# Row maxima spread through the vector engine's step, and the odd query stack copied on GpSimd

## What is computed

```
h = layernorm(x) * (1 + ca) + sa                 # ca, sa, ... from silu(c) @ wmod, one row per batch
a = h + proj(windowed_attention(layernorm(h)))   # 16 heads of 8, windows of 64 tokens that step by 32
a = a + mlp(layernorm(a))                        # 128 -> 512 -> 128 with gelu
x = x + ga * a
h = layernorm(x) * (1 + cb) + sb
x = x + gb * sum_e weight_e(h) * expert_e(h)     # 8 experts, silu(h Wg) * (h Wu) @ Wd
```

## Time and profile before

| | |
|---|---|
| median of 3 runs | 341.74 us (339.88 to 345.77) |
| the profiled execution | 342.37 us, its span 340.6 us |
| mean granted TensorE clock | 0.843 of full speed |
| busy share of the span | PE 83%, PEld 65%, DVE 66%, ACT 41%, POOL 23% |
| attention, 8 steps | about 54 to 217 us, some 20.5 us each |
| stack reads | 48 DMAs of 216 KB, median 4.8 us from issue to landing |

### The profile page before, as it was taken

How to read it: one execution, slowest core, us unless ns; L and a number is a source line. 1 busy time by engine, 2 the same in 40 slices (tenths; PEclk the granted TensorE clock), 3 DMA queues, 4 the chain that set the end, 5 groups by cost and what they waited for, 6 DMA issues and landing times.

```text
span 340.6 us, 10357 instructions
## 1 busy us (share of the span) xinstructions
PE 283.2 (83%) x4168; PEld 222.6 (65%) x4168; DVE 225.3 (66%) x634; ACT 141.0 (41%) x282; POOL 77.3 (23%) x116
## 2 busy tenths in 40 slices
PE   4855479599797898969798999887899989999992
PEld 2423356487675666747687787565697778878992
DVE  7564664645858368363745626498857898798986
ACT  1354136328364372635226235554537216624220
POOL 5453240311405015000101110125540024003020
PEclk9995559659789696997659556999979999999999
DMA  5109652286617346172610350000000000100001
GB/s 179 46 0 219 148 121 70 81 192 145 153 51 161 105 96 162 44 168 75 134 29 6 89 172 3 0 2 0 0 2 1 0 2 0 32 2 31 2 32 32
DMA packets 21902, 23.71 MB, mean 70 GB/s; under 512 B 3296, under 2 KB 18528, under 8 KB 21856
## 3 DMA queue, kind: packets, MB, share of 16 engines
q1 hardware_dynamic: 21856, 23.06, 27.4%
HBM read 14.67 MB, written 8.13 MB: 67 GB/s over the span
## 4 chain that ended last, share of the span: by engine, by line
PE 46%; DVE 18%; issue 9%; DMA 9%; SPq 9%; ACT 6%; POOL 3%; DVEq 0%; ACTq 0%; POOLq 0%
PE bank L655 6%; SPq L285 5%; PE bank L450 4%; PE bank L407 4%; DVE xh L1032 4%; DMA qst<-stack_scratch 3%; PE bank L440 3%; PE bank L392 3%; PE bank L430 3%; PE bank L637 3%; PE bank L371 3%; PE bank L639 3%; PE bank L638 3%; DMA qst<-mt 3%; DVE acc L1371 2%
## 5 line engine op out<-in xcount | busy, mean ns | idle before, releaser
L1073 DVE TENSOR_REDUCE nm<-bank 128x8 f32<-128x512 f32 x64 | 43.3, 689 | 29.6 <-PE bank L392 29.5
L740 ACT ACTIVATE prob<-bank 128x512 f32<-128x512 f32 x64 | 36.4, 599 | 28.0 <-PE bank L407 27.6
L878 POOL TENSOR_TENSOR rs<-ve,mhalf 128x2 f32<-128x2 f32 (+1 forms) x24 | 19.8, 827 | 122.6 <-DVE ve L1029 115.7
L392 PE MATMUL bank<-kst,qst 48*64 48x64 bf16 x1024 | 32.0, 211 | 9.3 <-issue 4.0
L392 PEld LDWEIGHTS bank<-kst,qst 48*64 48x64 bf16 x1024 | 25.1, 123 | 18.8 <-issue 13.1
L830 ACT ACTIVATE sg<-bank 128x512 f32<-128x512 f32 x32 | 18.9, 601 | 43.6 <-PE bank L639 42.1
L655 PEld LDWEIGHTS bank<-wds,hh 128*128 128x128 f32 x256 | 32.3, 191 | 7.0 <-issue 5.3
L655 PE MATMUL bank<-wds,hh 128*128 128x128 f32 x256 | 33.7, 277 | 2.7 <-DVE acc L1371 2.3
L407 PE MATMUL bank<-qst,kst 50*64 50x64 bf16 x1024 | 30.2, 210 | 5.2 <-DMA qst<-mt 4.7
L1371 DVE SCALAR_TENSOR_TENSOR acc<-bank,rt,acc 128x128 f32<-128x128 f32 x112 | 32.6, 341 | 1.2
L430 PE MATMUL bank<-prob,vb 128*32 128x64 f32 x1024 | 27.3, 255 | 6.8 <-issue 4.2
(11 more groups left out here) (140 smaller groups left out, 517.5 us busy)
## 6 DMA issues: line engine op xcount, KB each, us to landing
qst<-stack_scratch SPq DMA_DIRECT2D x32, 216.0 KB, 4.8
stack_scratch<-parts SPq DMA_DIRECT2D x16, 216.0 KB, 2.5
kst<-stack_scratch SPq DMA_DIRECT2D x16, 216.0 KB, 4.9
stack_scratch<-parts SPq DMA_DIRECT2D x16, 144.0 KB, 2.4
stack_scratch<-parts SPq DMA_DIRECT2D x16, 72.0 KB, 3.0
qst<-mt SPq DMA_DIRECT2D x64, 4.0 KB
out_x<-fin SPq DMA_DIRECT2D x4, 256.0 KB, 2.3
xs<-in_x SPq DMA_DIRECT2D x1, 896.0 KB, 7.3
```

The source lines that it names most:

```text
L392: m = pe.matmul(psa[g % 2][WIN * half:WIN * half + WIN, WIN * h2:WIN * h2 + WIN], qst[n][eo][rows_, h2, at:at + WIN], kst[n][rows_, h2, at ...
L740: act.activation(prob[g // 2 % 2][:, :, g % 2, :], psb[g % 2][:].rearrange("p (h q) -> p h q", h=H2), ACT.Exp).then_inc(exp_done, 1)
L1073: dve.tensor_reduce(nm[:, g, :], psa[g % 2][:].rearrange("p (h k) -> p h k", h=H2), AX_X, ALU.max, negate=True).then_inc(max_done, 1)
```

## The change

Three edits. The maxima are placed at other points of DVE's step, and with them ln_b and copy_mt(b + 1, 0). The second read of the query stack is taken out, and GpSimd copies the even stack's columns to the odd stack instead (`copy_odd`), with a semaphore of its own; scores_a of groups 0 to 3 waits for four DMAs and that of groups 4 to 7 for the copy. The copy covers 112 partitions, also those between the two halves, so DVE zeroes 32 partitions of each even query stack once at the start (three more memsets of the same shape as the six of `kst`).

```diff
@@ sync, read_stacks
-                for k, stack, written in ((0, qst[n][0], q_written), (1, kst[n], k_written),
-                                          (0, qst[n][1], q_written)):
+                for k, stack, written in ((0, qst[n][0], q_written), (1, kst[n], k_written)):
@@ sync, start
-            sp.wait_ge(ones_ready, after(ones_ready, 2 * DEEP))
+            sp.wait_ge(ones_ready, after(ones_ready, 3 * DEEP))
@@ tensor, scores_a
-                pe.wait_ge(stack_ready, after(stack_ready, 96 * (b + 1)))
+                if g < 4:
+                    pe.wait_ge(stack_ready, after(stack_ready, 64 * (b + 1)))
+                else:
+                    pe.wait_ge(odd_ready, after(odd_ready, b + 1))
@@ gpsimd
+            def copy_odd(b):
+
+                pool.wait_ge(stack_ready, after(stack_ready, 64 * (b + 1)))
+                even, odd = [qst[b % DEEP][eo][0:64 + ROWS, :, LINE - S:LINE] for eo in range(2)]
+                pool.tensor_copy(odd, even).then_inc(odd_ready, 1)
...
             copy_x1v(1)
+            copy_odd(0)
             cut_m(0, 0)
@@ gpsimd, step(b)
                 if b + 1 < B:
                     cut_m(b + 1, 0)
+                if b == 0:
+                    copy_odd(1)
...
                     second_root_x(b + 4)
+                if 0 < b < B - 2:
+                    copy_odd(b + 2)
                 if b + 1 < B:
                     cut_m(b + 1, 1)
+                if b == 0:
+                    copy_odd(2)
@@ vector, start
                     dve.memset(kst[n][64 * par + 32:64 * par + 64].bitcast(F32), TWO_ONES).then_inc(ones_ready, 1)
+                dve.memset(qst[n][0][32:64].bitcast(F32), 0.0).then_inc(ones_ready, 1)
@@ vector, step(b)
                 maxima_next(2)
+                if norm:
+                    ln_b(b + 4)
                 maxima_next(3)
                 if group is not None:
                     ln2_stats(group)
                 normalise(b, 0)
-                if norm:
-                    ln_b(b + 4)
+                if ahead:
+                    copy_mt(b + 1, 0)
+                maxima_next(4)
                 if prep:
                     cut_qk(b + 3, 0)
-                if ahead:
-                    copy_mt(b + 1, 0)
+                maxima_next(5)
                 if prep:
                     cut_qk(b + 3, 1)
                 if group is not None:
                     normed_tokens(group)
-                maxima_next(4)
+                maxima_next(6)
                 if not ahead:
                     gate(GA)
                 if norm:
                     ln_c(b + 4)
-                maxima_next(5)
-                maxima_next(6)
                 maxima_next(7)
```

More of the change, by code:

```diff
@@ L197, in build @@
         stack_ready = sem("stack_ready")
+        odd_ready = sem("odd_ready")
         v_done, v_ready = sem("v_done"), sem("v_ready")
```

## The result

| | before | after |
|---|---|---|
| median of the runs | 342.35 us (4 runs, 339.88 to 345.77) | 352.69 us (4 runs, 350.10 to 355.14) |
| profiled execution, its span | 342.37, 340.6 us | 355.14, 353.3 us |
| mean granted TensorE clock there | 0.843 | 0.808 |
| step 0 begins (first copy_mt of a step) | 54.69 us | 58.75 us |
| seven steps, to the same copy of step 7 | 146.3 us | 154.3 us |

The ratio of the times is 1.0364, with a 95% interval from 1.0295 to 1.0433: the change made the kernel slower, by 10.3 us between the medians and by some 12 us by the ratio, where I had forecast 338 us with a range of 332 to 345.

What follows compares the result with a forecast made beforehand. It took the attention as a PE program with holes, neither PE-bound nor DMA-bound. Start +2.5 and steps 1 to 4 -6.4 made -3.9 us on the profiled 342.37, so 338.5, or 338 us against the median; range 332 to 345.

Steps and rivals of the forecast that it cites:

- the costing of copy_odd: POOL's copy taken as 2.4 us, between second root and cut_m(b + 1, 1), hidden from transpose_m with 2.1 us left.
- Rival 2: PE's clock stays at 2.4 GHz without the holes of steps 1 to 4: 5 us shorter, 333 us; chance 0.22.
- The start: Before step 0: three more memsets, partly offset by an earlier first stack; net +2.5 us, ends +3.9 and +1.5.
- +3.9: At the start: three more memsets of 1.31 us each delay DVE's first dependent instruction by 3.9 us.
- -1.4: At the start: fewer reads let PE begin scores_a(0, 0) 2.4 us sooner, of which 1.4 us come back at m0.
- Steps 1 to 4: Earlier m4, maxima's rows and code block close PE's holes: gains 1.1, 2.0, 1.2 and 2.1 us, sum -6.4 us.
- The reads and the code: probs_v's "issue" holes are code queued behind stack reads; four reads bring it 2.2 us sooner, holes under 1 us.
- rival 1: "Issue" holes not tied to the reads: step 2 gains 1.0 us, step 4 nothing, 341 us; chance 0.2.
- it does not bind: Step 2: DVE keeps pace, normalise(b, 1) from 112.1 against 114.41, 2.3 us sooner, within a gain of about 2.0.
- Step 0: No gain; copy_odd(1) delays scores_a(1, 4) by 2.4 us, under PE's 3.35 us stall for ACT, which waits for write_parts.
- Rival 3: POOL late: copy takes 5.3 us, delaying steps 0 to 3; 344 us, decisive from 4.5 us a copy; chance 0.08.
- Rival 4: The start costs its full 3.9 us and the steps give 3 only: 342 to 343 us; chance 0.1.

Runs made afterwards that it cites:

- e11: e9 plus, on GpSimd where copy_odd had stood, same-shape copies that no other engine waits for; 348.41 us, ratio 1.0269 to the kernel before.
- e5: Changed kernel with the copies of steps 1 to 5 moved behind cut_m(b + 1, 1) and made to wait for ctxn; 340.02 us, ratio 1.0001 to the kernel before.
- e7: Changed kernel with copy_odd made by ScalarE in its idle stretches instead of GpSimd; 335.58 us, no ratio.
- e9: Changed kernel with copy_odd on ScalarE and the three added memsets in VectorE's idle places, more rounds than e8; 333.56 us, ratio 0.9875 to the kernel before.
- e1: Kernel before with only DVE's new order, keeping six reads a batch and six memsets; 340.52 us, ratio 0.9972.
- e2: Changed kernel with DVE's old order put back, keeping the GpSimd copy, four reads and added memsets; 345.32 us, no ratio.
- e12: Changed kernel with 22 matmuls on ones in place of 5 ahead of gather_context in steps 1 to 4; 343.91 us, ratio 1.0128 to the kernel before.
- e3: Kernel before with only the three more memsets added at DVE's head; 346.39 us, ratio 1.0108.
- e4: Changed kernel with its three added memsets moved from the head into DVE's idle places; 349.57 us, ratio 1.0199 to the kernel before.
- e8: Changed kernel with copy_odd on ScalarE and the three added memsets in VectorE's idle places; 335.75 us, no ratio.
- e10: e9 with DVE's old order put back; 338.65 us (328.94 to 352.64, 12 runs), no ratio.
- e6: Changed kernel with every GpSimd copy of batches 3 to 7 made twice in the same place; 352.87 us, ratio 1.044 to the kernel before.

## Why the prediction was wrong, point by point

**The step that failed** is the costing of copy_odd: "So it is hidden with 2.1 us left." I asked only how late POOL would be. The copy's length was over-estimated on the safe side (1.89 us, where I took 2.4 from a range of 1.8 to 5.3), cut_m followed it at once, and no transpose_m waited for it. But while it ran, it held DVE's instructions between SBUF operands, and one of these, fac, stands on the path from turn_sums to gather_context. My own working had both at the same moment, "112.1 to 114.5" for the copy and "normalise(b, 1) from 112.1", and I did not put the two lines side by side. I had even seen a DVE cast go from 0.46 to 0.78 us beside POOL and applied that factor to the copy, the wrong side: the one that starts later is the one that is held, and it is held to the end. Shown by e11 (the copy's presence alone costs it), e5 (place) and e7 to e9 (another engine). e1 and e2 show the order's part: by itself it costs nothing, but it brought fac of steps 1 to 3 under the copy.

The Trainium skill, "SBUF — State Buffer", section "Who interferes with whom", states this as a rule: GpSimd and VectorE share one pair of ports as an exclusive lock, which an instruction keeps for its whole length, and of VectorE's instructions those in a two-port mode need it, and so do those with two SBUF inputs when GpSimd's instruction reads SBUF, as this copy does. The traces agree with it: fac and qkr (two SBUF inputs) were held to the copy's end, the copy and the maximum out of PSUM were not. Section 8 of the Trainium skill, "GPSIMD Engine Reference", which the prediction cites, names the same two kinds of VectorE instruction as in contention with GpSimd; the prediction kept only the one with both ports, took the harm to fall on both, and did not look for one with two SBUF inputs behind ve.

**The size of it: the clock.** Rival 2 had the clock as a thing to gain when holes close. The holes I named did close, all of them; that a new hole of 2.9 us at another place would put a whole step at 1.2 GHz was not in any case. Its size is known only roughly. PE's busy time for the same matmuls is 5.4 us higher after the change, and in e12 it is 5.0 us lower again, with 68 matmuls more. The whole effect of e12 is about 8 of the 12 us, from ratios of 1.0364 and 1.0128 whose intervals just touch (1.0295 and 1.0311), and it has step 5 in it, which the added matmuls do not explain. So 5 us are the clock as far as shown, and what is over stays open.

**The start.** "+3.9" was right for DVE's first dependent instruction (3.7). "-1.4" was right as far as PE goes (2.8 us of the 3.7 came back before scores_a(0, 0), 2.4 were forecast), and failed on DVE for the same reason as above: copy_odd(0) begins at 39.32, held x1h until 41.29 and with it m0, which in the earlier trace rows had waited for PE. The sum at step 0 was +4.1 and not +2.5; of it the memsets alone have 1.95 (e3), and without them at the head it is gone (e4, -0.9).

**Steps 1 to 4.** m4 next to copy_mt, no stall before scores_a 6: right, in the changed kernel and e1. **The reads and the code**: right as far as tested. The holes stand at fixed instructions: that of step 4 with 9 matmuls of its probs_v left in the kernel before, e1, e3 and e7, that of step 2 with 17 left in the kernel before, e3, e8 and e9, whatever their length. This fits the reading as a boundary of code and no wait. With six reads the hole in step 4 is 2.75, 2.75 and 2.47 us (before, e1, e3), with four 0.55 (e7) or none (changed kernel, e2), so rival 1's "step 4 nothing" falls. But the reads are not all of it: step 2's hole went in e1 with six reads, e12 has 1.45 and 2.03 us with four, and the 1.14 us of step 7 in the changed kernel, over the 1 us that I had set as a sign, come behind other DMA traffic (share 0.94 from 212 to 214 us). Ahead of e12's 2.03 us the DMA share was 0.15 only (154 to 156 us). So what sets the length of such a hole stays open, and I had priced it by the end of the reads alone. But -6.4 us was the sum of four closed holes, as if nothing stood close behind them. In e1 the same PE program ran into waits for the maxima's rows and for ctxn, of 1.41 and 1.19 us, and gained nothing; step 2's "it does not bind" was wrong even without a copy. Only e9 against e10 hints that the order pays once the reads are four.

**Step 0.** I had copy_odd(1) hidden under PE's stall for ACT. It was. PE waited 2.00 us for the copy and then 2.95 us more for ACT's parts, where it had waited 3.35, but the end of this wait is set by ACT, and ACT was late by itself. ACT in order of time, step 0 before:

```profile
62.73 0.50 ACT L716 ACTIVATE qk<-bank,bqs 128x288 f32<-128x288 f32 x1 [4.42 <-DMA stack_scratch<-parts]
```

After:

```profile
68.46 0.50 ACT L719 ACTIVATE qk<-bank,bqs 128x288 f32<-128x288 f32 x1 [6.10 <-DMA stack_scratch<-parts]
```

Against the first copy_mt of the step, ACT goes on 1.7 us later than before, and PE's transposes come 1.7 us later too. It waits for the landing of write_parts, which comes 3.1 us behind the last issue where it came 1.6 behind it. The copy on GpSimd is not shown as its cause: e10, with no copy there, has 3.1 as well, and e11, with one, 2.1. So 1.7 of the step's 2.3 us stay open.

**Rivals 3 and 4** were the ones on the side of slower. Rival 3 had the copy's place right and the victim wrong: it made cut_m late at over 4.5 us a copy, and at 1.89 us it was out of play. Rival 4 had a start of 3.9 us (4.1 measured), but still with a gain of 3 in the steps. To more than 348.6 us I had given 0.04.

**What stays open.** In step 5 scores_b waits 3.33 us for the maxima's rows (1.82 before); e9 has 1.54 there and e12 0.97. SP issued those rows from 171.22 us and the stack reads behind them; no run took this wait apart.

## What to carry to other kernels

Before work is moved to GpSimd, list what VectorE does in that same stretch: each of its instructions between SBUF operands may have to wait for the whole of one GpSimd instruction, whatever its own size, so a short one on the path to TensorE can cost as much as the longest thing GpSimd runs (0.19 us became 1.78 behind a copy of 1.89). Here the copy did no harm on ScalarE, which had idle time for it; otherwise it belongs behind the short instruction, by a wait if the order alone does not ensure it. And price a hole in TensorE's work twice, as the wait itself and as what follows at 1.2 GHz; a few matmuls on constants across the wait can cost less than the low clock behind it (e12).

## What the runs showed of the hardware that was not expected

- A GpSimd copy of 112 x 2048 bf16 takes 1.89 us, about as long as the memset of 2048 float32 in the earlier trace rows (1.80). The Trainium skill, "GPSIMD Engine Reference", section 3.1, gives 1.03 cycles an element for bodies of at most two operations, an estimate of 1.76 us at 1.2 GHz, and the trace is near it. The prediction had set its figure for a tight unrolled loop, 3.1 us, beside the sum. ScalarE takes 1.91 us for the same copy.
- The hold is that of one instruction: of two GpSimd copies 0.06 us apart, fac waited out only the first, and x1h the second (e6).
- The hold can fall on GpSimd. In e4 the copy at 159.86 took 2.56 us: it started 0.07 us ahead of a qkr that took its usual 0.73. Starts so close do not tell which of the two is held: in e6 a fac that starts 0.03 us behind a copy, at 166.15, was held for 1.90.
- About 1.6 us added to one VectorE instruction five times, with two more at the start and at 181 us, cost 15 us between the medians of e9 and e11, in their profiled executions the larger part through TensorE's clock.
- TensorE, busy without a break from 102 to 125 us, stayed at a granted clock of 0.50 all that time.
